# Expanded map in groups of 32 channels instead of 16, and the order of the front convolution that goes with it

## Time and profile before

| | |
|---|---|
| median of 3 runs | 2807.51 us (2800.09 to 2807.88) |
| the profiled execution | 2798.28 us, of which the span is 2796.5 us |
| PE (TensorE) busy | 2339.4 us (84%) |
| DVE (VectorE) busy | 1596.0 us (57%) |
| ACT (ScalarE) busy | 1013.3 us (36%) |
| POOL (GpSimd) busy | 536.7 us (19%) |
| DMA, SyncE's queue (q1) | 417490 packets, 418.23 MB, 57.0% of the 16 engines' span |
| `y<-exp_out` | 64 DMAs of 816 KB, 12.3 us from issue to landing |
| `gate_data<-y` | 24 DMAs of 2176 KB, 15.2 us |
| `gate_wt<-wm` | 96 DMAs of 256 KB, 4.8 us |
| `g<-gate_out` | 48 DMAs of 578 KB, 3.6 us |

### The profile page before, as it was taken

The page is one execution under the profiler, slowest core; times in us unless marked ns, Lnnn a source line. Parts: engine busy times, 40 slices in busy tenths (PEclk is TensorE's granted clock), DMA queues, the critical chain, the costliest instruction groups (busy, mean ns, idle before and its releaser), DMA issues. The chain is left out here.

```text
span 2796.5 us, 62141 instructions
## 1 busy us (share of the span) xinstructions
PE 2339.4 (84%) x21290; PEld 1273.4 (46%) x21290; DVE 1596.0 (57%) x2838; ACT 1013.3 (36%) x1923; POOL 536.7 (19%) x833
## 2 busy tenths in 40 slices
PE   5767749999969999997399999999994999688887
PEld 2333438777743333331156666666662232233332
DVE  3334411111127777775078888888882445477776
ACT  3344411111118888884100000000000112377776
POOL 7510000000000000003055555665550000000000
PEclk9888869999989999996579999999997899799999
DMA  6987888777737777774655555555543999433332
GB/s 140 249 224 208 212 250 276 267 266 261 270 91 137 147 147 147 147 143 99 133 117 129 123 129 132 130 129 121 130 107 87 229 250 267 120 102 107 103 104 79
DMA packets 550647, 454.97 MB, mean 163 GB/s; under 512 B 335272, under 2 KB 464480, under 8 KB 547136
## 3 DMA queue, kind: packets, MB, share of 16 engines
q1 hardware_dynamic: 417490, 418.23, 57.0%
q10 hardware_dynamic: 129024, 15.75, 4.8%
q0 software_dynamic: 4032, 19.53, 2.9%
HBM read 270.23 MB, written 183.74 MB: 162 GB/s over the span
## 5 line engine op out<-in xcount | busy, mean ns | idle before, releaser
L556 PE MATMUL gate_ps<-gate_data,gate_wt 64*64 64x289 f32 x6144 | 384.3, 408 | 53.2 <-DMA gate_data<-y 39.6
L556 PEld LDWEIGHTS gate_ps<-gate_data,gate_wt 64*64 64x64 f32 x6144 | 311.9, 133 | 125.6 <-issue 60.3
L875 ACT CAST mix_h<-mix_bank 96x512 f16<-96x512 f32 x512 | 267.6, 593 | 7.0 <-PE mix_bank L826 3.2
L596 DVE TENSOR_TENSOR gate_out<-gate_gelu,gate_ps 128x578 f32<-128x578 f32 x96 | 72.6, 757 | 345.0 <-PE gate_ps L556 339.4
L1137 POOL MEMSET cg_image<- 48x7680 f32 x1 | 6.5, 6491 | 1131.7 <-POOLq L58 1131.7
L286 DVE COPY exp_out<-exp_y 128x384 f32<-128x384 f32 x192 | 102.8, 567 | 154.6 <-PE exp_y L249 153.0
L573 ACT ACTIVATE gate_gelu<-gate_ps 128x578 f32<-128x578 f32 x96 | 62.7, 653 | 351.6 <-PE gate_ps L556 351.6
L2012 PE MATMUL fus_bank<-fus_xt,fus_taps 76*32 76x512 f32 x1344 | 159.5, 626 | 27.2 <-DMA fus_shift<-gate_shift 24.3
L957 DVE TENSOR_SCALAR mix_hb<-mix_h,mix_b1q 96x1024 f16<-96x1024 f16 x256 | 122.7, 479 | 93.6 <-ACT mix_h L875 93.6
L826 PE MATMUL mix_bank<-mix_xq,mix_w1q 112*96 112x512 fp8e5 x512 | 143.5, 382 | 29.1 <-ACT mix_h L875 23.0
L965 DVE CAST mix_hq<-mix_hb 96x2048 fp8e5<-96x2048 f16 x128 | 156.5, 1223 | 19.8 <-DVE mix_hb L957 17.9
(11 more groups left out here) (220 smaller groups left out, 4316.8 us busy)
## 6 DMA issues: line engine op xcount, KB each, us to landing
y<-exp_out SPq DMA_DIRECT2D x64, 816.0 KB, 12.3
gate_data<-y SPq DMA_DIRECT2D x24, 2176.0 KB, 15.2
g<-gate_out SPq DMA_DIRECT2D x48, 578.0 KB, 3.6
mix_sc<-g SPq DMA_DIRECT2D x31, 816.0 KB
gate_wt<-wm SPq DMA_DIRECT2D x96, 256.0 KB, 4.8
wav_strips<-xp SPq DMA_DIRECT2D x96, 204.0 KB, 2.9
wav_halves<-xp SPq DMA_DIRECT2D x48, 340.0 KB, 4.4
wav_conv<-wav_lines ACTq DMA_DIRECT2D x384, 40.0 KB
```

The lines of the kernel that those rows point to most:

```text
L556: mm = pe.matmul(banks(a, v)[64 * g:64 * (g + 1), r], wt[q][64 * r:64 * (r + 1), 2 * a + g, n, :], src, start=n == 0, stop=n == 3)
L875: act.copy(h16[at.pair][:, m, h, :], bank[(2 * m + h) % len(bank)][0:HID, :]).then_inc(h16_ready, 1)
```

## The change

The group becomes 32 channels (16 of each half), so `y` is written in runs of 2176 bytes, and its image pair u becomes the second axis, so that one image pair of a group lies in one piece. `gated_conv` has 6 groups; one of its two data buffers now holds one image pair of 32 channels (rows of 34816 bytes, one DMA of 4352 KB). The order becomes: for each group, image pair v = 0 with steps q = 0 to 7, then image pair v = 1 with the same eight. Eight weight tiles and eight output tiles are resident (four and two before). In a step TensorE runs a = 0 and then a = 1 for one image pair, and the PSUM and gelu buffers alternate with q. SyncE stores and reloads weights only in the second half of a group, when an output tile has both image pairs; the next group's first data is queued ahead of these, its second behind. At the start SyncE waits for the first data before it queues weights 2 to 7 and the second data.

```diff
-GRP = 16
+GRP = 32
...
-                            dst = t["y"][:, h, :, u, bass.ds(i + N * s, 1)].rearrange("g p o w -> p g (o w)")
+                            dst = t["y"][:, u, h, :, bass.ds(i + N * s, 1)].rearrange("g p o w -> p g (o w)")
...
-    GROUPS, QUADS = HID // 8, 4
+    GROUPS, STEPS = O2 // GRP, GRP // 4
...
-        data = [k.sb(f"data{p}", [128, LEAD + (2 * (BX + 1) + 1) * ROW]) for p in range(2)]
-        wt = [k.sb(f"wt{q}", [128, 4, 4, P8 * P8]) for q in range(QUADS)]
+        data = [k.sb(f"data{v}", [128, LEAD + (BX + 2) * ROW]) for v in range(2)]
+        wt = [k.sb(f"wt{q}", [128, 4, 4, P8 * P8]) for q in range(STEPS)]
...
-        out = [k.sb(f"out{p}", [128, BX + 1, B, BX + 1]) for p in range(2)]
+        out = [k.sb(f"out{q}", [128, BX + 1, B, BX + 1]) for q in range(STEPS)]
...
+        def step(i, v, q):
+            return 2 * STEPS * i + STEPS * v + q
...
-                def load_data(i, p):
-                    src = t["y"][bass.ds(2 * i + p, 1)].rearrange("o r p v y w -> (o r p) v (y w)")
-                    rows = data[p][:, LEAD:].rearrange("q (y w) -> q y w", w=ROW)
-                    for v in range(2):
-                        at = 1 + (BX + 1) * v
-                        sp.dma_start(rows[:, at:at + BX].rearrange("q y w -> q (y w)"), src[:, v]).then_inc(data_in[p], 16)
+                def load_data(i, v):
+                    src = t["y"][bass.ds(i, 1), v].rearrange("o r p y w -> (o r p) (y w)")
+                    sp.dma_start(data[v][:, LEAD + ROW:LEAD + (BX + 1) * ROW], src).then_inc(data_in[v], 16)
...
+                def store(i, q):
+                    sp.wait_ge(out_ready, step(i, 1, q) + 3)
...
                 load_weights(0, 0)
                 load_data(0, 0)
-                for q in range(1, QUADS):
-                    load_weights(q, q)
+                load_weights(0, 1)
+                sp.wait_ge(data_in[0], 16)
+                for q in range(2, STEPS):
+                    load_weights(0, q)
                 load_data(0, 1)
...
+                with sp.Fori(0, GROUPS - 1) as i:
+                    sp.wait_ge(out_ready, step(i, 0, STEPS - 1) + 3)
+                    load_data(i + 1, 0)
+                    for q in range(STEPS):
+                        store(i, q)
+                        load_weights(i + 1, q)
+                    load_data(i + 1, 1)
...
+                with pe.Fori(0, GROUPS) as i:
+                    for v in range(2):
+                        for q in range(STEPS):
+                            e, j = q % 2, step(i, v, q)
                             if q == 0:
-                                pe.wait_ge(data_in[p], 32 * i + 32)
-                            pe.wait_ge(wt_in[q], 32 * (2 * i + p) + 32)
+                                pe.wait_ge(data_in[v], 16 * i + 16)
+                            if v == 0:
+                                pe.wait_ge(wt_in[q], 32 * i + 32)
                             for a in range(2):
...
+                                            at = LEAD - 1 + ny * ROW + (GRP // 2 * a + 2 * q + g) * (BX + 1) + nx
...
-        "winT": inp["L0_conv_w_in"].reshape(2, HID // 8, 8, C).transpose(3, 1, 0, 2).reshape(C, O2),
+        "winT": inp["L0_conv_w_in"].reshape(2, O2 // GRP, GRP // 2, C).transpose(3, 1, 0, 2).reshape(C, O2),
...
-    "y": (HID // 8, 2, P8 * P8, 2, BX, GRP * (BX + 1)), "wm": (HID // 2, P8 * P8, 2, 2, 4 * P8 * P8),
+    "y": (O2 // GRP, 2, 2, P8 * P8, BX, GRP * (BX + 1)), "wm": (HID // 2, P8 * P8, 2, 2, 4 * P8 * P8),
```

More of the change, by code:

```diff
@@ L500, in load_weights @@
                                      ).then_inc(wt_in[q], 16)
[L502 to L508, removed]
+                def store(i, q):
+                    sp.wait_ge(out_ready, step(i, 1, q) + 3)
+                    sp.dma_start(t["g"][bass.ds(2 * STEPS * i + 2 * q, 2)].rearrange("c p w -> (c p) w"),
+                                 out[q][:, :, :, :].rearrange("p w b x -> p (w b x)")).then_inc(stored[q], 16)
+                for q in range(STEPS):
+                    sp.sem_inc(stored[q], 16)
                 sp.wait_ge(cleared, 1)
@@ L541, in _ @@
                             for a in range(2):
[L542 to L560, removed]
@@ new lines, in _ @@
+                                if a == 0:
+                                    pe.wait_ge(gelu_ready, j + 1)
+                                else:
+                                    pe.wait_ge(out_ready, j + 1)
+                                pe.sem_inc(pe_turn, 1)
+                                for n in range(4):
+                                    ny, nx = n // 2, n % 2
+                                    for r in range(2):
+                                        for g in range(2):
+                                            at = LEAD - 1 + ny * ROW + (GRP // 2 * a + 2 * q + g) * (BX + 1) + nx
+                                            first = data[v][64 * r:64 * (r + 1), at:at + 1]
+                                            src = bass.AP(first.tensor, first.offset,
+                                                          [list(first.ap[0]), [ROW, BX + 1], [1, BX + 1]])
+                                            mm = pe.matmul(
+                                                banks(a, e)[64 * g:64 * (g + 1), r],
+                                                wt[q][64 * r:64 * (r + 1), 2 * a + g, n, :], src,
+                                                start=n == 0, stop=n == 3)
@@ L565, in _ @@
                 act.sem_inc(gelu_ready, 2)
[L566 to L573, removed]
+                with act.Fori(0, GROUPS) as i:
+                    for v in range(2):
+                        for q in range(STEPS):
+                            j = step(i, v, q)
+                            act.wait_ge(summed[0], j + 1)
+                            act.wait_ge(out_ready, j + 1)
+                            act.activation(gelu[q % 2][:, :, :], banks(0, q % 2), ACT.Gelu).then_inc(gelu_ready, 1)
@@ L575, in _ @@
             @block.vector
             def _(dve):
-                for p in range(2):
-                    dve.memset(data[p][:, 0:LEAD + ROW], 0.0)
-                    for y in (BX + 1, 2 * (BX + 1)):
-                        last = dve.memset(data[p][:, LEAD + y * ROW:LEAD + (y + 1) * ROW], 0.0)
+                for v in range(2):
+                    dve.memset(data[v][:, 0:LEAD + ROW], 0.0)
+                    last = dve.memset(data[v][:, LEAD + (BX + 1) * ROW:LEAD + (BX + 2) * ROW], 0.0)
```

70 lines of the change are left out of this document (28 added, 42 removed).

## The result

The changed kernel takes 2805.85 us (median of 20 runs, 2801.61 to 2818.34). The kernel before, timed again beside it, takes 2799.13 (median of 20 runs, the three shown above among them and on its slow side; 2777.35 to 2822.74, and one of 7951.21). The ratio of the two, which leaves out the three runs of before that lie more than 1.5% above its fastest, is 1.0043, 95% interval [1.0022, 1.0063]: a small loss, clear of noise, where a gain of 17 us was forecast. The profiled execution took 2802.55 us, its span 2800.8.

A forecast was written before the change was run, and what follows sets the result against it. Transfers were taken to bound `expand`, TensorE the convolution. Savings of 5.8 + 3.8 + 1.9 + 3 + 2 - 0.5 = 16 us, rounded to 17, took the median from 2807.5 to 2790.5 us; range 2750 to 2807.

The forecast's parts named there:

- the term for the convolution: First to last matmul of the gated convolution: same matmul records, passes and five pauses of 13.7 us, so no change.
- Stores of `expand`: Longer rows save 0.96 us a turn: 5.8 us from 44 to 195 us, 3.8 in later pairs, 1.9 in the tail.
- the sharing: In `expand`, longer packets give SyncE's queue more against GpSimd's `wm` traffic, which moves into later idle time: 3 us.
- The pairs: Four later pairs of turns in `expand`, bound by the u = 0 stores ahead of the load: 0.96 us each, 3.8 us.
- the tail: End of `expand`, where two turns' stores drain against nothing: 1.9 us saved (0 to 7).
- The mixed queue: Stretch of a turn in `expand` with stores and loads queued together: forecast to run at over 300 GB/s.
- the lonely stores: First stores of a turn's u = 0 in `expand`, alone in the queue: 210 GB/s before, forecast 210 to 220.
- the forecast's last 1 us: Rounding the sum from 16 to 17 us, since a shorter stall lets a turn or two start at the higher clock.
- Start: Start of the convolution: less competition for its first weights and data saves 2 us (0 to 4).
- The cover: Convolution's transfers: a second half's load and eight pairs of store and weights run over 10.6 us, leaving 10.8 us spare.
- rival 3: Convolution: the second half of a group starves TensorE as data 1 is late; 48 us lost, 2838 us; chance 7%.
- Wider row step: Convolution's matmuls: the wider row step costs TensorE nothing; a record above 402 ns would show otherwise.

The follow-up runs named there:

- e6: The changed kernel with each store of the expanded map cut in two along the row, giving runs of 1088 bytes; 2825.36 us (one run).
- its control: The changed kernel with each store of the expanded map cut in two between groups, keeping runs of 2176 bytes; 2808.73 us (one run).
- e1: The changed kernel without the reload of weights inside the convolution's loop, all groups using those of group 0; 2810.78 us (one run).
- e3: The changed kernel with only TensorE's convolution loop rotated by half a group, so its branch falls after a first half; 2777.67 us.
- e2: The kernel before with an unused extra load of a group's data queued some 7 us ahead of each pass's end; 2828.72 us (one run).

## Why the prediction was wrong, point by point

- **Sign and cause.** The forecast was faster, with 7% on slower, for starvation of TensorE. The loss came from somewhere else. The step that failed is the term for the convolution, held at nothing: "The convolution itself: ... five pauses of 'issue' at the passes' ends, 13.7 us. Nothing, but it hangs on the transfers". I had the row of the pauses, and further down I had worked out that the transfers of a second half run 10.6 us over into the next first half. The end of a half is the end of a pass. I priced that overhang against data and weights only, not against the one other thing that uses the DMA engines there, TensorE's own code. The measured price is 11.5 us of pauses (25.2 in place of 13.7) and 6.6 us of passes run partly at the lower clock: 18.1 us where the sum had nothing.
- **The median.** 2805.85 lies inside 2750 to 2807 only at its end; the rerun of before, 2799.13, shows that the base of 2807.5 was 8 us high. The sum against the profiled execution's 2798.3 was the better base.
- **Stores of `expand`.** Forecast 5.8 + 3.8 + 1.9 us, with 3 for the sharing: 14.5. The two traces show 14.3, the means over several executions 9, e6 against its control 15.7. So 14.3 against 14.5 in the one pair of traces was luck; over several executions the sum was some 5 us too high, and the error is in the early terms: 5.8 + 3 for the stores ahead of 195 us and the sharing came to 3.5. The pairs gave 1.3 us each where 0.96 was forecast (an estimate of 13 ns a packet, had all of it been fixed cost, against the 10 taken), the tail 2.1 against 1.9. Waits for `exp_xt` fell to 66.6, not 60; the later four to 4.95 to 5.99, as forecast. The mixed queue should have passed 300 GB/s and stayed where it was (272 before, 276 after), the lonely stores gained 5%, as the forecast said of 210 to 220.
- **The clock beside the sum.** No run shows the 1.2 GHz. The traces give the clock as a share of full speed, 0.52 from 254 to 262 us before, and the forecast's last 1 us rests on that and on the cold turn's 16.65 us against 15.4.
- **Start.** 16.36 us from the issue against 16 to 17 forecast, and 18.89 before. Over several executions the two kernels are 17.7 and 16.8, so 1 us of the 2.
- **The cover.** The second half's load and eight pairs did run over as worked out: the engines idle from 472 us, 19 us into the first half, where 22.4 was forecast. No wait for data, weights or output tiles: rival 3 did not happen, and its "no wait for `gate_data` behind the first" was the right sign to read. The output tiles' stores landed in time.
- **Wider row step.** 403 ns a matmul record: nothing, as held.
- **What would have found it.** The forecast listed "idle time still about 14 us" as a sign. It should have asked what ends a pause of 2.6 to 3.0 us that no semaphore explains, and whether that thing is still alone there.

## What to carry to other kernels

A branch of TensorE's loop, with 1024 matmul records to a pass, cost 1.8 to 3.0 us here beside idle DMA engines and 4.5 to 6.2 beside full ones, and no pause was left with the loop written out. In a kernel whose trace shows such pauses, try the branch where the transfer queue is short, or write the loop out on the engine that sets the pace. When transfers are regrouped into bursts, list everything that meets the burst, packets of code as well as data. And for stores that reach half of the partitions, getting both halves into flight moved the rate more than the row length did: 272 GB/s with finer turns and up to 362 with two queues, where doubling the rows gave 221. But read the time as well as the rate: the finer turns cost SyncE issue time, and the pairs of turns hardly got shorter.

## What the runs showed of the hardware that I had not expected

- TensorE's branch back costs 1.8 to 3.0 us with idle DMA engines (before, e1, e3: a share of at most 0.09 in the 2 us behind the last matmul) and 4.5 to 6.2 us with full ones (after, e2, e6 and its control: at least 0.98), over 34 branches; the packet of code that TensorE's return follows comes 2 to 3 us later then. Written out, 6144 matmul records take 378.2 to 379.3 us against 392.7 to 418.2 with the loop.
- Two queues filled what one didn't: 362 GB/s with each half of the partitions on its own queue. For streams of stores these runs show 221 GB/s from one queue with 816 KB turns, 272 with 272 KB turns, and up to 362 from two queues, though only in three of six turns.
- Doubling a row of 1088 bytes gave 5% to stores that reached half of the partitions, and nothing clear to a mixed queue (272 and 276 GB/s over the first 10 us), and yet the stage got 9 us shorter in the mean, of which 3.8 lie in three pairs of turns. That small gains where the engines are full add up to this is my reading; the runs separate row length from DMA count, and no run isolates the part ahead of 217 us.
